# A three-block decoder on one core: every third Mamba state's product with B moved to GpSimd, from a copy of B in SBUF, with a new order table

## The chip, the cores and the metric

The kernel runs on one core of one Trainium2 chip. The metric is device time in microseconds (us), from the start of the program to its end. A profiled execution gives a trace with every instruction; its span is from the first to the last instruction.

## The reference

Four batches of 512 tokens of width 128 go through six blocks, each followed by a layer norm: a Mamba block, a cross attention of 16 heads, a mixture of experts, a window attention, a second cross attention, and a block of two layers of local attention with a gated feed-forward. The change lies in the Mamba block, whose scan is this:

```python
def step(h, inp):
    d_t, b_t, c_t, u_t = inp
    dA = jnp.exp(d_t[..., None] * A)
    dBu = d_t[..., None] * b_t[:, None, :] * u_t[..., None]
    h = dA * h + dBu
    y_t = jnp.einsum('bdn,bn->bd', h, c_t)
    return (h, y_t)
```

There are 256 channels and 16 states (index n). For each state the decay is exp(delta * A), the input is (delta * u) * B with B of that state, and the output adds h * C with C of that state.

## The kernel before

**Lanes and rounds.** The work of four batches is done in two lanes with buffers of their own (row buffers 0 and 1). Each lane computes two batches, one after the other (two rounds), and each batch goes through the six blocks. The two lanes run side by side: on each engine one instruction stream holds both lanes' instructions. Stage functions such as `mamba_tensor`, `mamba_scalar`, `mamba_vector` and `mamba_pool` are Python generators; each `yield` ends a step. `interleave` merges the lanes' steps by the table `TURNS`, which has a list of numbers for each engine: so many steps of lane 0, then so many of lane 1, and so on. The engines run their streams strictly in order, and semaphores tie them together. So `TURNS` is an order written out as numbers, for the whole kernel, and any new step in a lane shifts what the numbers mean behind it.

**The state loop.** Channels are two blocks (c = 0, 1) of 128 partitions; time (512 tokens) lies along the free axis. For each state n and each lane:

- TensorE spreads B of the state over all partitions (line 617, a selecting matmul of bf16 parts into PSUM), and later C of the state in the same way. Both go through one PSUM bank per lane (`t.v.use(1)`), so C can be written only when B has been read, and the next B only when C has been read.
- VectorE multiplies delta*u by B out of PSUM, both blocks in one instruction of 128x1024 (line 757), into `dBu[n % 2]`.
- ScalarE makes the decay exp(delta*A) of block 0 into one PSUM bank per lane (line 693, `dA`); VectorE runs the scan of block 0 (line 765, 128x512), which frees `dA`; then the same for block 1. So a lane's second exponential waits for its first scan, and the first of the next state for its second scan.
- ScalarE copies C out of PSUM into `Cs[n % 2]` (line 699).
- GpSimd multiplies the states of both blocks by C (line 796, 128x1024) into `hC[n % 2]`.
- TensorE adds `hC` to the sums in PSUM by two fp32 matmuls with the identity (line 623), which the trace shows as four records.

Buffers `hs`, `dBu`, `Cs` and `hC` are double: the scan of state n waits for GpSimd's product of state n-2, GpSimd's product of state n for the sum of n-2.

In the unrolled table of before, once the loop is under way, VectorE has two products (one of each lane) and then four scans, and so on. TensorE has, in the same stretch: C of one lane, C of the other, two sums, B of one, B of the other.

Behind the loop, lines 772 and 776 finish a lane's output, line 634 projects it, line 561 adds the residual; ahead of it, lines 741 to 746 make delta and delta*u. Later stages that the prediction speaks of: the cross attention behind Mamba (line 812 is its first matmul), the experts (lines 919, 963, 1008), the window attention (line 1115).

Of the kernel before, what the change touches and what calls it, by code (L numbers as in the profile page):

```python
# [32 lines left out]
P = 128  # L33
# [12 lines left out]
DEPTH = 2  # L46
EPS = 1e-5
# [35 lines left out]

TURNS = {
# [17 lines left out]
    "act": [  # L102
# [13 lines left out]
    "dve": [  # L116
# [21 lines left out]
    "pool": [  # L138
# [103 lines left out]
def decoder_kernel(nc, x_in, packed, cb_in, experts_in, folded_dram, out):  # L242
    with ExitStack() as ctx:
# [27 lines left out]
        def again(of, at=0):  # L271

            used[of] = at
# [1563 lines left out]
```

## Time and profile before

| | us |
|---|---|
| median of three runs | 1657.88 |
| lowest and highest of these | 1654.49 and 1671.53 |
| the profiled execution, its own time | 1675.55 |
| its span | 1673.8 |
| TensorE busy in it | 1360.8 (81%) |
| VectorE busy | 1076.3 (64%) |
| ScalarE busy | 807.2 (48%) |
| GpSimd busy | 328.3 (20%) |
| mean granted TensorE clock | 0.909 |

The shares are means over stages with different limits. The granted clock is given as a share of 2.4 GHz: 1.00 is 2.4 GHz all the time, 0.50 is 1.2 GHz. Lines of a trace name an instruction by its line in the kernel; "scratch" is the large SBUF buffer that holds most tiles of the stages.

### The profile page before, as it was taken

Reading aid. Unit: us, or ns where it says so; the run is one execution under the profiler, and the core shown is the slowest. Engines: PE = TensorE matmul, PEld = TensorE weight load, DVE = VectorE, ACT = ScalarE, POOL = GpSimd, SP = SyncE. Lnnn points to the kernel's source line nnn. Section 1 sums busy time; section 2 is a strip of 40 time slices with the busy share of each in tenths; the row PEclk is TensorE's granted clock in tenths of the full one; section 3 lists DMA queues with packets and bytes.
Section 4 is the critical chain, followed back from the end, with each engine's and each line's share of the span. In section 5 each row is a group of like instructions: output and inputs, shape, how many; then the busy total and the mean of one; then the engine's idle time right before and its main releaser. Section 6 shows DMA issues by size and latency. Waiting matters only on the chain. (4 is left out here: it accounts for less than half of the span.)

```text
span 1673.8 us, 23084 instructions
## 1 busy us (share of the span) xinstructions
PE 1360.8 (81%) x8604; PEld 858.4 (51%) x8604; DVE 1076.3 (64%) x2223; ACT 807.2 (48%) x2040; POOL 328.3 (20%) x212
## 2 busy tenths in 40 slices
PE   6656778998899789788865766899979986878886
PEld 5212235776566446455631223467756654654672
DVE  5599964115687788357439898721378877843863
ACT  0555414432666256546526452343347635664663
POOL 0046620002000052033010565100110004202310
PEclk9769968999999989989877899899999998999798
DMA  7300000000000010001000000000000000100000
GB/s 290 151 0 1 0 1 26 0 1 1 1 2 2 7 39 20 1 13 27 1 25 1 0 1 1 13 14 1 1 1 2 2 1 14 24 3 13 14 14 13
DMA packets 12927, 30.89 MB, mean 18 GB/s; under 512 B 1425, under 2 KB 5905, under 8 KB 12562
## 3 DMA queue, kind: packets, MB, share of 16 engines
q1 hardware_dynamic: 8978, 23.14, 3.7%
q10 hardware_dynamic: 3840, 6.29, 1.6%
q8 instruction: 69, 1.13, 0.3%
q14 instruction: 40, 0.33, 0.1%
HBM read 17.89 MB, written 5.24 MB: 14 GB/s over the span
## 5 line engine op out<-in xcount | busy, mean ns | idle before, releaser
L796 POOL TENSOR_TENSOR scratch<-scratch 128x1024 f32<-128x1024 f32 x64 | 149.4, 2352 | 174.8 <-DVE scratch L765 170.6
L963 ACT ACTIVATE scratch<-psum,w_experts 128x512 f32<-128x512 f32 x144 | 98.0, 688 | 146.1 <-PE psum L919 142.6
L535 POOL TENSOR_SCALAR rstd<-mv 128x4 f32<-128x4 f32 x28 | 7.7, 274 | 814.9 <-DVE mv L522 814.9
L693 ACT ACTIVATE psum<-scratch,a_neg 128x512 f32<-128x512 f32 x128 | 88.6, 692 | 129.7 <-DVE scratch L765 124.0
L765 DVE TENSOR_TENSOR_SCAN scratch<-psum,scratch 128x512 f32<-128x512 f32 x128 | 147.4, 1206 | 2.4 <-ACT psum L693 2.3
L1008 DVE SCALAR_TENSOR_TENSOR y<-psum,comb,y 128x128 f32<-128x128 f32 x128 | 36.0, 345 | 169.8 <-PE psum L943 169.8
L943 PEld LDWEIGHTS psum<-expert_weights,scratch 128*128 128x128 f32 x1152 | 134.1, 192 | 17.6 <-issue 17.1
L623 PE MATMUL psum<-scratch,w_const 128*128 128x512 f32 x256 | 134.6, 668 | 8.7 <-POOL scratch L796 8.6
L943 PE MATMUL psum<-expert_weights,scratch 128*128 128x128 f32 x1152 | 135.3, 275 | 0.9 <-DVE y L1008 0.9
L919 PE MATMUL psum<-xT,expert_weights 128*128 128x512 f32 x288 | 134.8, 602 | 1.1 <-ACT scratch L963 1.1
L1447 ACT ACTIVATE scratch<-psum,mx 128x128 f32<-128x128 f32 x256 | 90.3, 375 | 89.1 <-DVE mx L1538 89.0
L617 PE MATMUL psum<-scratch,cb 96*128 96x512 bf16 x128 | 49.0, 417 | 90.4 <-DVE scratch L757 74.5
L1115 ACT ACTIVATE scratch<-psum,mx 128x256 f32<-128x256 f32 (+1 forms) x256 | 111.3, 458 | 20.4 <-DVE mx L1151 18.6
L1282 PE MATMUL psum<-w_local,hT 128*128 128x512 f32 x192 | 93.4, 631 | 7.3 <-ACT hT L1264 7.1
L536 POOL TENSOR_TENSOR small<-small,w_const 128x16 f32<-128x16 f32 x32 | 96.1, 3004 | 2.7
L623 PEld LDWEIGHTS psum<-scratch,w_const 128*128 128x128 f32 x256 | 53.8, 215 | 64.7 <-issue 45.6
L617 PEld LDWEIGHTS psum<-scratch,cb 96*128 96x128 bf16 x128 | 12.7, 100 | 141.0 <-DVE scratch L757 101.1
L757 DVE TENSOR_TENSOR scratch<-scratch,psum 128x1024 f32<-128x1024 f32 x64 | 75.6, 1213 | 11.6 <-PE psum L617 11.6
L1325 PE MATMUL psum<-scratch 64*64 64x128 f32 x512 | 81.7, 308 | 0.0
L1323 PE MATMUL psum<-scratch 64*64 64x128 f32 x512 | 81.7, 308 | 0.0
L535 POOL TENSOR_SCALAR small<-small 128x16 f32<-128x16 f32 x32 | 24.0, 750 | 293.9 <-DVE small L1492 293.9
L1151 DVE TENSOR_REDUCE mx<-psum 128x4 f32<-128x1024 f32 (+1 forms) x56 | 68.4, 1222 | 15.8 <-PE psum L1062 15.7
(228 smaller groups left out, 3070.3 us busy)
## 6 DMA issues: line engine op xcount, KB each, us to landing
scratch<-scratch ACTq DMA_DIRECT2D x48, 128.0 KB, 2.3
expert_weights<-in_expert_weights SPq DMA_DIRECT2D x9, 512.0 KB, 9.8
folded_products<-scratch SPq DMA_DIRECT2D x8, 512.0 KB, 2.7
folded<-folded_products SPq DMA_DIRECT2D x8, 512.0 KB, 3.4
w_local<-in_local SPq DMA_DIRECT2D x1, 3122.0 KB
scratch<-in_cross SPq DMA_DIRECT2D x1, 2624.5 KB, 8.9
x<-in_x SPq DMA_DIRECT2D x4, 256.0 KB, 3.5
out<-xT SPq DMA_DIRECT2D x4, 256.0 KB, 2.4
```

Of the source, the lines that this page charges most:

```text
L536: t.eng.tensor_tensor(dst, dst, W("const", "neg_half").to_broadcast([P, dst.shape[1]]), ALU.pow)\
L623: ins = pe.matmul(sum_banks[c], ident, t.m.hC[:, 2 * ((n - 1) % 2) + c, :], start=(n == 1), stop=(n == NS))
L693: act.activation(t.ps["dA"], t.m.delta[:, c, :], ACT.Exp, scale=a_neg[:, c, n:n + 1])\
L765: dve.tensor_tensor_scan(t.m.hs[:, n % 2, c, :], t.ps["dA"], t.m.dBu[n % 2][:, c, :], 0.0, ALU.mult, ALU.add)\
L796: t.eng.tensor_tensor(t.m.hC[:, 2 * (n % 2):2 * (n % 2) + 2, :], t.m.hs[:, n % 2], C, ALU.mult)\
L919: pe.matmul(t.a.open(), we[:, k, f * P:(f + 1) * P], t.m.xT[:, :], start=True, stop=True)\
L943: ins = pe.matmul(tok(bank, i), tok(t.m.hid[:, (k - 1) % 2, f, :], i), we[:, k - 1, FF + f * P:FF + (f + 1) * P], start=(k > 1 and i == 0 ...
L963: act.activation(t.m.hid[:, k % 2, f, :], t.a.take(), ACT.Gelu_apprx_tanh, bias=W("experts", "b1")[:, c:c + 1]).then_inc(t.s["a_freed"], 1)
L1115: ins = act.activation(t.m.wide_pr[:, n % 2, u, z], bank[:, z], ACT.Exp, bias=t.m.mx2[:, c:c + 1], accum_out=t.m.sums2[:, c:c + 1])
L1282: pe.matmul(ring.open(), tok(t.m.hT, i), w_qkv[:, c * 512:(c + 1) * 512], start=True, stop=True).then_inc(t.s[sig], 1)
L1323: pe.matmul(own[0:64, :], qs[:, 0:64], ks[:, q - before:q - before + P], start=False, stop=False, skip_group_check=True)
L1447: ins = act.activation(tok(t.m.pr[:, u, :], a), tok(bank, a), ACT.Exp, bias=t.m.mx2[:, c:c + 1], accum_out=t.m.sums2[:, c:c + 1])
```

## The change

For the states 2, 5, 8, 11 and 14 the product with B is taken from VectorE and given to GpSimd. GpSimd reads B from SBUF, so ScalarE first copies B out of PSUM into a new tile `Bs` (one per lane). In GpSimd's stream the product of state n+1 stands ahead of the product h*C of state n. In ScalarE's stream the copy of B stands ahead of the state's first exponential, and for every state the copy of C now stands between the two exponentials (before: behind both). A new semaphore `B_used` tells VectorE's scan and ScalarE's next copy of B that GpSimd's product is done. `TURNS` is new for all four engines and the whole kernel, both rounds.

```diff
+POOL_B = range(2, NS, 3)
...
+            m.Bs = carve(i, 1, T)
...
# mamba_scalar
             for n in range(NS):
+                if n in POOL_B:
+                    yield
+                    if n > POOL_B[0] or t.row:
+                        t.w(t.s["B_used"])
+                    act.activation(t.m.Bs[:, 0, :], t.v.take(), ACT.Copy).then_inc(t.s["v_freed"], 1)
+                else:
+                    t.skip(v=1)
                 for c in range(NB):
...
-                t.skip(v=1)
-                yield
-                if n >= 2:
-                    t.w(t.s["state_ready"])
-                act.activation(t.m.Cs[:, n % 2, :], t.v.take(), ACT.Copy).then_inc(t.s["v_freed"], 1)
+                    if c == 0:
+                        yield
+                        if n >= 2:
+                            t.w(t.s["state_ready"])
+                        act.activation(t.m.Cs[:, n % 2, :], t.v.take(), ACT.Copy).then_inc(t.s["v_freed"], 1)
# mamba_vector
-                if n >= 2:
-                    dve.wait_ge(t.s["decay_used"], NB * (NS * t.row + n - 1))
-                bank = t.v.take().rearrange("p (o z) -> p o z", o=1).to_broadcast([P, NB, T])
-                dve.tensor_tensor(t.m.dBu[n % 2], t.m.du[:, :, :], bank, ALU.mult).then_inc(t.s["v_freed"], 1)
+                if n in POOL_B:
+                    t.skip(v=1)
+                else:
+                    if n >= 2:
+                        dve.wait_ge(t.s["decay_used"], NB * (NS * t.row + n - 1))
+                    bank = t.v.take().rearrange("p (o z) -> p o z", o=1).to_broadcast([P, NB, T])
+                    dve.tensor_tensor(t.m.dBu[n % 2], t.m.du[:, :, :], bank, ALU.mult).then_inc(t.s["v_freed"], 1)
                 for c in range(NB):
-                    yield
+                    if c or n not in POOL_B:
+                        yield
                     if c == 0:
-                        dve.wait_ge(t.s["v_freed"], t.v.at)
+                        if n in POOL_B:
+                            t.w(t.s["B_used"])
+                        else:
+                            dve.wait_ge(t.s["v_freed"], t.v.at)
# mamba_pool
+            def product_B(n):
+                yield
+                if n == POOL_B[0]:
+                    t.w(t.s["delta_ready"])
+                t.eng.wait_ge(t.s["v_freed"], t.v.at + 1)
+                t.eng.wait_ge(t.s["decay_used"], NB * (NS * t.row + n - 1))
+                t.eng.tensor_tensor(t.m.dBu[n % 2], t.m.du, t.m.Bs.to_broadcast([P, NB, T]), ALU.mult)\
+                    .then_inc(t.s["B_used"], 1)
             for n in range(NS):
                 t.skip(v=2)
+                if n + 1 in POOL_B:
+                    yield from product_B(n + 1)
```

Unrolled, the new table gives these streams in the middle of the loop (first round, three states of both lanes). The digit ahead is the lane, the number the state; P is line 757, s a scan with its block a or b, e an exponential, C and BS the copies, hC and PB GpSimd's products with C and B, b TensorE's spreading of B (a) or C (b), sum line 623:

```
VectorE  1s8b 1P9 0s10b 1s9a 1s9b 1P10 0s11a 1s10a 0s11b 0P12 1s10b 0s12a 0s12b 0P13 1s11a 0s13a 1s11b
GpSimd   0hC9 1hC8 0PB11 0hC10 1hC9 0hC11 1PB11 1hC10 0hC12 1hC11
ScalarE  0BS11 1C9 0e11a 0C11 1e9b 1e10a 1C10 0e11b 1e10b 0e12a 1BS11 0C12 1e11a 1C11 0e12b 0e13a
TensorE  1b10a 1b10b 0sum10 0b12a 1sum9 1b11a 0b12b 1b11b 0sum11 0b13a 0b13b 1sum10 1b12a 0sum12
```

## Rows read from the trace of the kernel before

**Rows 1.** Busy time of each engine, stretches of the two state loops
```profile
core 0: us, PE busy (x) PEld busy (x) DVE busy (x) ACT busy (x) POOL busy (x), PEclk, DMA share, GB/s
120.00:160.00 40.00, 27.91 (x69) 10.63 (x68) 38.36 (x35) 21.11 (x36) 26.08 (x12) 0.97 0.00 1
...
960.00:1000.00 40.00, 27.50 (x71) 10.86 (x71) 40.00 (x37) 21.68 (x36) 27.32 (x12) 1.00 0.00 1
```

**Rows 2.** Timeline of VectorE, one period (start, length, line, count)
```profile
151.44 2.35 DVE L757 TENSOR_TENSOR scratch<-scratch,psum 128x1024 f32<-128x1024 f32 x2
153.70 4.56 DVE L765 TENSOR_TENSOR_SCAN scratch<-psum,scratch 128x512 f32<-128x512 f32 x4
158.21 1.22 DVE L757 TENSOR_TENSOR scratch<-scratch,psum 128x1024 f32<-128x1024 f32 x1
```

**Rows 3.** Timeline of TensorE, the same period
```profile
153.84 0.39 PE L617 MATMUL psum<-scratch,cb 96*128 96x512 bf16 x1 [0.74 <-DVE scratch L757]
154.07 3.60 PE L623 MATMUL psum<-scratch,w_const 128*128 128x512 f32 x8
157.50 0.60 PE L617 MATMUL psum<-scratch,cb 96*128 96x512 bf16 x2
```

**Rows 4.** Timeline of VectorE, fourth to fifteenth state of both rounds
```profile
115.94 2.33 DVE L757 TENSOR_TENSOR scratch<-scratch,psum 128x1024 f32<-128x1024 f32 x2
124.39 2.35 DVE L757 TENSOR_TENSOR scratch<-scratch,psum 128x1024 f32<-128x1024 f32 x2 [1.64 <-PE psum L617]
...
193.50 2.33 DVE L757 TENSOR_TENSOR scratch<-scratch,psum 128x1024 f32<-128x1024 f32 x2
...
933.26 2.33 DVE L757 TENSOR_TENSOR scratch<-scratch,psum 128x1024 f32<-128x1024 f32 x2
...
943.03 2.35 DVE L757 TENSOR_TENSOR scratch<-scratch,psum 128x1024 f32<-128x1024 f32 x2 [2.96 <-PE psum L617]
...
1012.33 2.35 DVE L757 TENSOR_TENSOR scratch<-scratch,psum 128x1024 f32<-128x1024 f32 x2
```

**Rows 5.** Busy time and clock, two stretches of 4 us
```profile
120.00:124.00 4.00, 4.00 (x8) 1.41 (x7) 2.75 (x3) 3.05 (x6) 2.29 (x1) 0.68 0.00 0
936.00:940.00 4.00, 4.00 (x6) 1.69 (x5) 4.00 (x4) 2.92 (x5) 1.94 (x2) 0.50 0.00 0
```

**Rows 6.** Timelines of GpSimd and ScalarE in the loop
```profile
136.96 4.67 POOL L796 TENSOR_TENSOR scratch<-scratch 128x1024 f32<-128x1024 f32 x2 [2.11 <-DVE scratch L765]
134.68 0.69 ACT L693 ACTIVATE psum<-scratch,a_neg 128x512 f32<-128x512 f32 x1 [2.74 <-DVE scratch L765]
135.31 0.58 ACT L699 ACTIVATE scratch<-psum 128x512 f32<-128x512 f32 x1
135.80 0.69 ACT L693 ACTIVATE psum<-scratch,a_neg 128x512 f32<-128x512 f32 x1
```

**Rows 7.** Timeline of VectorE where line 746 meets GpSimd's first product
```profile
89.81 1.22 DVE L744 TENSOR_TENSOR scratch<-scratch 128x1024 f32<-128x1024 f32 x1
95.45 2.48 DVE L746 TENSOR_TENSOR scratch<-scratch 128x1024 f32<-128x1024 f32 x1
```

**Rows 8.** Stage ends by line, first round (to 906), then second (ns; first and last start)
```profile
L765 DVE TENSOR_TENSOR_SCAN scratch<-psum,scratch x64: 1194/1202/1224, 91.0 to 212.0; 128x512 f32<-128x512 f32 x64
L1008 DVE SCALAR_TENSOR_TENSOR y<-psum,comb,y x64: 339/344/352, 297.2 to 408.5; 128x128 f32<-128x128 f32 x64
L1115 ACT ACTIVATE scratch<-psum,mx x128: 358/473/547, 427.7 to 543.0; 128x256 f32<-128x256 f32 x96, 128x128 f32<-128x128 f32 x32
...
L765 DVE TENSOR_TENSOR_SCAN scratch<-psum,scratch x64: 1193/1201/1224, 908.8 to 1030.4; 128x512 f32<-128x512 f32 x64
L1008 DVE SCALAR_TENSOR_TENSOR y<-psum,comb,y x64: 335/344/352, 1103.1 to 1220.2; 128x128 f32<-128x128 f32 x64
L1115 ACT ACTIVATE scratch<-psum,mx x128: 359/474/548, 1235.7 to 1346.6; 128x256 f32<-128x256 f32 x96, 128x128 f32<-128x128 f32 x32
```

More of the change, by code:

```diff
@@ L387, in decoder_kernel @@
                      "stats_ready rstd_ready norm_ready score_loaded e_ready prob_ready pT_used x_loaded "
-                     "squares_ready rms_ready u_ready soft_ready delta_ready parts_ready decay_ready decay_used state_ready states_used "
+                     "squares_ready rms_ready u_ready soft_ready delta_ready parts_ready decay_ready decay_used state_ready states_used B_used "
                      "sum_filled sums_read gated_ready gap_ready ratio_ready comb_ready pads_ready "
```

106 rows, old and new, of the table TURNS are left out of this document.

## Prediction

> **What bounds the kernel now.** The change lies in the state loop, which runs twice, once a round; so I read the busy time of each engine in stretches of the loop first, where the page's shares over the whole span would mislead. VectorE works 38.36 of 40 us in the first round's loop and 40.00 of 40 in the second's; TensorE is at 28, GpSimd at 26 and 27, ScalarE at 21 [rows 1]. That says VectorE. The timeline of one period says how closely another bound follows. A period is one state of both lanes: two products with B, then four scans, from 151.44 to 158.21, so 6.77 us, with no idle time between them [rows 2]. The steps between starts are 1.13 for a product and 1.128 for a scan: (158.21 - 153.70) / 4. Beside it runs a chain through TensorE: the second product ends at 151.44 + 2.35 = 153.79, TensorE starts C at 153.84, the eight records of the two sums from 154.07, the next two B at 157.50, which take 0.60 [rows 3]; that ends at 158.10, and the next product starts at 158.21. So product, C, two sums, B and product again also make 6.77. The loop has two bounds of one length, and taking away VectorE's work alone frees only one of them.
>
> The second one shows where the granted clock falls. From the fourth state's pair of products to the fifteenth's are 193.50 - 115.94 = 77.56 us in the first round and 1012.33 - 933.26 = 79.07 in the second, for 11 states each [rows 4]: 7.05 and 7.19 a state, and not 6.77. Two of the stalls stand in the rows, 1.64 and 2.96 us, both on line 617; the granted clock in the stretches ahead of them is 0.68 and 0.50 [rows 5], so wholly or partly at 1.2 GHz. Over 22 states this costs 156.63 - 22 x 6.77 = 7.7 us.
>
> **The change, by the engine's own work.** I count three states of both lanes, since the pattern repeats after three; one round has five such patterns and a state more.
>
> VectorE now has 6 products and 12 scans, 6 x 1.13 + 12 x 1.128 = 20.3 us. Two products go: 18.05. Over both rounds 5 states x 2 lanes x 2 = 20 products go, 22.6 us of VectorE. That is the most which VectorE's own work can give.
>
> GpSimd has 6 products with C; two back to back take 4.67 [rows 6], 2.335 each. The new product has the same shape, 128x1024 fp32 from two SBUF operands, so I take the same duration. Eight make 18.7 us: GpSimd, that idled a third of the time, becomes the fullest engine, above VectorE's 18.05. Nothing shorter than 18.7 is possible.
>
> ScalarE has 12 exponentials at a step of 0.63 and 6 copies at 0.49 (135.31 - 134.68 and 135.80 - 135.31) [rows 6], 10.5 us; two more copies of B make 11.5. It doesn't fill up, but its stream is in order, which matters next.
>
> **The change, by what waits for what.** I laid the four new streams side by side and followed who must wait. GpSimd's product of lane 1's state 8 waits for that state's second scan. Behind it, in one stream, are lane 0's product with B of state 11, lane 0's product with C of state 10 and lane 1's product with C of state 9: four in a row. The last of them is awaited by TensorE's sum of state 9 of lane 1, and TensorE's spreading of B for state 11 of lane 1 stands behind that sum. On it waits ScalarE's copy of B, and behind the copy in ScalarE's stream stand the copy of C of lane 0's state 12, lane 1's exponential of 11, a copy of C, and the second exponential of lane 0's state 12. On that waits VectorE's scan; behind that scan stand lane 0's product 13, lane 1's scan of 11, lane 0's of 13, and the second scan of lane 1's state 11, for which GpSimd waits in turn. So the circle closes after three states. Its length:
>
> - GpSimd: 4 x 2.335 = 9.34 [rows 6]
> - TensorE: four records of a sum at (157.50 - 154.07) / 8 = 0.43, 1.72, and B, 0.39: 2.11 [rows 3]
> - ScalarE: 0.49 + 0.49 + 0.63 + 0.49 + 0.69 = 2.79 [rows 6]
> - VectorE: a scan, a product and two scans by their steps, 4.51, and the last scan in full, about 1.18: 5.69 [rows 2]
> - four hand-overs between engines: 0.05 (153.79 to 153.84) and 0.11 (158.10 to 158.21) are the two seen [rows 2, 3]; at 0.08 each, 0.3
>
> Sum 20.2 us for three states, 6.75 a state, beside 6.77 now. GpSimd then idles 1.5 us in three states and VectorE 2.2, though neither has a lack of work. So at the full clock I expect the loop not to gain from the 22.6 us that VectorE sheds: the wait for the product with B is replaced by one for GpSimd, handed on through sum, B and copy.
>
> What does gain is the loop's dependence on TensorE's clock. Now the circle holds a C, two sums and two B a period, all twice as long at 1.2 GHz, some 4.2 us in 6.77, 12.7 in three states; after the change 2.1 in 20.2. If the clock dips as it does now, the 7.7 us shrink by 2.1 / 12.7, to about 1.3. For the 22 states: 22 x 6.75 + 1.3 = 149.8 instead of 156.6, -6.8 us.
>
> The other ten states (the first four of each round, and the last) run with parts of the prologue and at a low clock. The new streams start with a product with B of state 2 ahead of GpSimd's product with C of state 1: late for lane 0's sum, early for its scan. I take nothing, with bounds of 3 us either way a round (half a period).
>
> The copy of C between the exponentials costs its 0.49 us ahead of each second exponential, but that one waits for its first scan (2.74 us of idle time before an exponential [rows 6]), so it lies in idle time: nothing, and up to 0.5 a state if that cover is gone; it gives C to GpSimd about one exponential earlier, for which nothing waits.
>
> One place costs. Line 746 took 2.48 us at 95.45, its like, line 744, 1.22 at 89.81 [rows 7]; GpSimd's first product ran in the same time. After the change GpSimd has a second product right behind it. Between nothing and 2.3 us a round, I take 0.5, so +1.0.
>
> By the Trainium skill ("SBUF — State Buffer", Who interferes with whom) a VectorE instruction with two SBUF inputs blocks against a GpSimd instruction that reads SBUF, and one with at most one SBUF input doesn't. By that rule line 746 may be held once more, and the scans and products of the loop, whose other input is in PSUM, never are. The trace agrees as far as GpSimd is now busy: the scans stay within 1.193 to 1.224 us in all 128 [rows 8]. If a fuller GpSimd held them up all the same, the loop would be slower than I say.
>
> **The order elsewhere.** The table is new for the whole kernel, and nothing else changes there. What an order can do is seen in the trace itself, since the two rounds do the same work by different lists. From the last scan to the experts' last instruction are 408.5 - 212.0 = 196.5 us in the first round and 1220.2 - 1030.4 = 189.8 in the second; the window attention from there 134.5 and 126.4 [rows 8]. I compared the lists by counting, for each step of lane 1, the steps of lane 0 ahead of it. In the window attention the new lists of both rounds lie within 1 to 2 steps of the old second round's on ScalarE and VectorE, and 3 to 6 from the old first round's. So the first round may gain up to 8.1 us there. Part of it is chance of the clock; I take half, -4. In cross attention and experts the new lists on TensorE lie nearer to the old first round's (some 5 steps) than to the second's (some 14), so the second round may lose up to 6.7; but the experts fill TensorE whatever the order. I take nothing, with bounds of -7 and +7.
>
> **Sum.** -6.8 + 1.0 - 4 = -9.8 us. Against the profiled execution's own 1675.55 (span 1673.8 and 1.75 around it) this gives 1665.7. That execution lies 17.7 us above the median of the runs, 1657.88; the same difference on the median gives 1648.1, my forecast. About 1% (16.6 us) is what a measurement of this kernel can tell from no change, since three runs before spread over 17 us.
>
> **The rivals.**
>
> *GpSimd is the bound, not the circle.* If hand-overs are shorter than I sum, or the streams slip against each other so that copy and sum are met earlier, three states take 18.7, 6.23 a state. Then 22 x (7.12 - 6.23) = 19.6 us go, and at half of that a state for the other ten, 4.5: with the window's -4 and the +1, 1631. For it: GpSimd's stream needs only 1.5 us less waiting in three states. Against it: each step of the circle is a fixed place in an in-order stream.
>
> *The new order elsewhere is worse.* The lists differ most in cross attention and experts. If both rounds lose there what now separates the rounds, 2 x 6.7 = 13.4, and the window gains nothing, then 1657.9 - 6.8 + 1 + 13.4 = 1665.5. It decides from about 6 us of loss. For it: the second round's list, the better one, is given up. Against it: TensorE is nearly full there.
>
> *Waits grow on the way.* If each hand-over costs 0.3 us instead of 0.08 (GpSimd's are seen on no tight path here), the circle is 21.1, 7.04 a state, and the loop gains 1.7 us over 22 states: 1653.
>
> **How the numbers follow.** Forecast 0.43, GpSimd the bound 0.27, the order worse 0.18, longer waits 0.12. The range 1626 to 1671 reaches past the first rival on one side (start of the loop 3 us a round better) and past the second by a part of its bounds on the other. Faster by over 1% means under 1641.3: nearly all of the first rival and a little of the forecast, 0.32. Slower by over 1% means over 1674.5: the tail of the second, 0.11. Within 1%: 0.57.
>
> **What would show it.** In the changed kernel's trace: GpSimd's busy time up by 20 x 2.35 = 47 us, to about 375; VectorE's down by about 24. From pair to pair three states apart 20.2 us if the circle holds, 18.7 if GpSimd is the bound: then its timeline has products without idle time. The waits should show the sum (line 623) waiting for GpSimd, line 757 no longer for line 617, and VectorE idle about 2 us in three states. The stage ends of rows 8 tell the order's part: the first round's window attention should be near 130. Wrong it would be if the loop's 11 states take under 72 us or over 78, or if the stages outside move by over 10 us in sum.

## The result, and the profile after

The changed kernel takes 1674.01 us, median of 16 runs (1659.67 to 1680.51); the kernel before 1662.32 in 16 runs of its own. The ratio is 1.0054, with a 95% interval of 1.0034 to 1.0075: slower by half a per cent, some 9 us, where I had forecast 9.8 us faster. The median lies above my range of 1626 to 1671. Part of that is the starting point: the forecast stood on three runs with a median of 1657.88, and 16 runs of the same kernel now give 4.4 us more. The direction was wrong all the same.

The page of the changed kernel gives for each engine its busy time, its share of the span and its number of instructions (PEld is TensorE loading weights):

```profile
PE 1375.6 (82%) x8604; PEld 867.0 (52%) x8604; DVE 1053.1 (63%) x2203; ACT 821.4 (49%) x2060; POOL 378.5 (23%) x232
```

The move did what it says. VectorE has 20 instructions and 23.2 us less, GpSimd 20 more and 50.2 us more, ScalarE 20 copies more. TensorE is the odd one: the same 8604 matmul records, and 14.8 us more in them (13.7 in the second profiles of both, told of below).

The page's groups of the loop (busy, mean ns | idle time ahead and what ended it); line 829 is GpSimd's product with C, 786 the scan, 630 the sum, 707 the exponential, 624 the spreading of B and C:

```profile
L829 POOL TENSOR_TENSOR scratch<-scratch 128x1024 f32<-128x1024 f32 x64 | 151.2, 2379 | 95.6 <-DVE scratch L786 95.5
L786 DVE TENSOR_TENSOR_SCAN scratch<-psum,scratch 128x512 f32<-128x512 f32 x128 | 150.0, 1209 | 26.1 <-ACT psum L707 25.4
L630 PE MATMUL psum<-scratch,w_const 128*128 128x512 f32 x256 | 142.0, 683 | 14.3 <-POOL scratch L829 13.0
L707 ACT ACTIVATE psum<-scratch,a_neg 128x512 f32<-128x512 f32 x128 | 88.5, 693 | 51.6 <-DVE scratch L786 48.9
```

The page of the kernel before has this for the scan:

```profile
L765 DVE TENSOR_TENSOR_SCAN scratch<-psum,scratch 128x512 f32<-128x512 f32 x128 | 147.4, 1206 | 2.4 <-ACT psum L693 2.3
```

VectorE idled 2.4 us ahead of scans and now idles 26.1 us, waiting for exponentials. That is 23.7 us more, about what it has given away (22.6 us of products).

The stage ends by line, as in [rows 8], first round and then second:

```profile
L786 DVE TENSOR_TENSOR_SCAN scratch<-psum,scratch x64: 1191/1214/1225, 88.6 to 205.1; 128x512 f32<-128x512 f32 x64
L1041 DVE SCALAR_TENSOR_TENSOR y<-psum,comb,y x64: 335/343/352, 290.6 to 404.5; 128x128 f32<-128x128 f32 x64
L1148 ACT ACTIVATE scratch<-psum,mx x128: 357/472/543, 419.8 to 533.0; 128x256 f32<-128x256 f32 x96, 128x128 f32<-128x128 f32 x32
...
L786 DVE TENSOR_TENSOR_SCAN scratch<-psum,scratch x64: 1191/1216/1225, 900.0 to 1020.8; 128x512 f32<-128x512 f32 x64
L1041 DVE SCALAR_TENSOR_TENSOR y<-psum,comb,y x64: 336/343/351, 1114.9 to 1220.4; 128x128 f32<-128x128 f32 x64
L1148 ACT ACTIVATE scratch<-psum,mx x128: 357/472/545, 1235.8 to 1350.1; 128x256 f32<-128x256 f32 x96, 128x128 f32<-128x128 f32 x32
```

From the last scan to the experts' end are 404.5 - 205.1 = 199.4 us and 199.6, against 196.5 and 189.8 before. The window attention takes 128.5 and 129.7, against 134.5 and 126.4.

One profile of a kernel is one execution, so I took a second of each. In this table every stretch is worked out from the stage ends as above: "loop" is from the first product with B of lane 0 to the start of the last scan, "to experts' end" from there to the start of the experts' last instruction.

| us | loop, round 1, 2 | to experts' end | window | span |
|---|---|---|---|---|
| before, two profiles | 124.6, 123.9; 122.5, 123.6 | 196.5, 189.8; 193.8, 189.7 | 134.5, 126.4; 134.5, 125.8 | 1673.8; 1664.8 |
| changed, two profiles | 120.0, 123.0; 119.8, 123.2 | 199.4, 199.6; 199.4, 199.5 | 128.5, 129.7; 128.5, 129.7 | 1672.8; 1666.2 |

The changed kernel's stretches come again to 0.2 us; of the kernel before, the first round's loop and the stretch behind it differ by 2.1 and 2.7 us. The local layers further on differ more (in the first round 276.3 and 271.2 us before, 281.2 and 274.3 changed). In the mean of two profiles the spans of the two kernels are equal (1669.3 and 1669.5), so single profiles can't carry a difference of 9 us; the runs do.

### The profile page after: what moved, and what is told of

Same layout as the page of the kernel before. It is cut to its first block and busy times, and to the rows that moved or that the text cites. A ratio compares the mean times of both kernels' runs of the same rounds, so it can differ in the third digit from the quotient of the medians.

```text
span 1672.8 us, 23122 instructions
## 1 busy us (share of the span) xinstructions
PE 1375.6 (82%) x8604; PEld 867.0 (52%) x8604; DVE 1053.1 (63%) x2203; ACT 821.4 (49%) x2060; POOL 378.5 (23%) x232
## 5 line engine op out<-in xcount | busy, mean ns | idle before, releaser
L786 DVE TENSOR_TENSOR_SCAN scratch<-psum,scratch 128x512 f32<-128x512 f32 x128 | 150.0, 1209 | 26.1 <-ACT psum L707 25.4
L630 PE MATMUL psum<-scratch,w_const 128*128 128x512 f32 x256 | 142.0, 683 | 14.3 <-POOL scratch L829 13.0
L976 PEld LDWEIGHTS psum<-expert_weights,scratch 128*128 128x128 f32 x1152 | 137.7, 196 | 15.3 <-issue 14.8
L976 PE MATMUL psum<-expert_weights,scratch 128*128 128x128 f32 x1152 | 138.6, 280 | 0.0
L1315 PE MATMUL psum<-w_local,hT 128*128 128x512 f32 x192 | 99.5, 666 | 6.8 <-ACT hT L1297 6.4
L952 PEld LDWEIGHTS psum<-xT,expert_weights 128*128 128x128 f32 x288 | 51.2, 190 | 50.0 <-issue 45.8
L624 PEld LDWEIGHTS psum<-scratch,cb 96*128 96x128 bf16 x128 | 13.1, 102 | 123.0 <-DVE scratch L774 71.7
## 6 DMA issues: line engine op xcount, KB each, us to landing
x<-in_x SPq DMA_DIRECT2D x4, 256.0 KB, 3.5
out<-xT SPq DMA_DIRECT2D x4, 256.0 KB, 2.4
```

What stands on the lines that cost most here:

```text
L630: ins = pe.matmul(sum_banks[c], ident, t.m.hC[:, 2 * ((n - 1) % 2) + c, :], start=(n == 1), stop=(n == NS))
L786: dve.tensor_tensor_scan(t.m.hs[:, n % 2, c, :], t.ps["dA"], t.m.dBu[n % 2][:, c, :], 0.0, ALU.mult, ALU.add)\
L952: pe.matmul(t.a.open(), we[:, k, f * P:(f + 1) * P], t.m.xT[:, :], start=True, stop=True)\
L976: ins = pe.matmul(tok(bank, i), tok(t.m.hid[:, (k - 1) % 2, f, :], i), we[:, k - 1, FF + f * P:FF + (f + 1) * P], start=(k > 1 and i == 0 ...
L1315: pe.matmul(ring.open(), tok(t.m.hT, i), w_qkv[:, c * 512:(c + 1) * 512], start=True, stop=True).then_inc(t.s[sig], 1)
```

## The experiments

Each run is compared with the kernel before on the same chip, by 4 to 11 executions of the edited kernel; the runs came in four batches on four chips, and ratios of different batches are compared only by way of the kernel before.

**Splitting order and loop.** Three kernels take the old order in one part and the new one in the other. Nothing but the numbers of `TURNS` differs.

```diff
 e1: TURNS: new inside both state loops, old everywhere else (changed code)
 e2: TURNS: old inside both state loops, new everywhere else (code before)
 e3: TURNS: new, but old in cross attention and experts      (changed code)
```

> The changed kernel with its new order only inside the two state loops; ahead of, between and behind them the four engines keep the old order. Theory A (the loop gains a little, the new order elsewhere costs more): from the first product with B to the last scan 120 to 123 us a round (124.6 and 123.9 before), the stretch from the last scan to the experts' last instruction back at about 196 and 190 us (199.4 and 199.6 in the changed kernel), and the whole faster than the kernel before, ratio 0.994 to 0.999. Theory B (the loop itself is what costs, or the two profiles differ by the clock alone): ratio near 1.005, as the changed kernel.

> The other half: the kernel before with its old code and old order in the state loops, and the new order everywhere else. Theory A: slower than the kernel before by more than the changed kernel is, ratio 1.006 to 1.012, with the last scan to the experts' end at 199 us in both rounds. Theory B: ratio 1.000 within 0.002.

> The changed kernel with the old order in cross attention and experts alone (both rounds); loops, window attention and all behind it keep the new order. Theory A in its narrow form (the cost sits in cross attention and experts, 2.9 and 9.8 us in the two profiles): ratio 0.996 to 1.000, the stretch at about 196 and 190 us. If the cost of the new order is spread over the later stages: ratio 1.003 or above.

> The kernel before once more, for a second profile of it. If stage lengths are set by the order, each stretch between stage ends comes again within 2 us of the first profile (loop 124.6 and 123.9, cross attention and experts 196.5 and 189.8, window 134.5 and 126.4). If they are set by when the clock falls, they scatter by as much as the two kernels differ (3 to 10 us).

Measured: the new loop in the old surroundings 1.0054 (1.0027 to 1.0080), the old loop in new surroundings 1.0042 (1.0017 to 1.0067). Each half alone costs about half a per cent, and both together, the changed kernel, no more than one of them. So the parts don't add. Theory A, as I had put it, falls by the first run (0.994 to 0.999 expected) and misses the second (1.006 to 1.012); Theory B falls by the second, since it wanted 1.000 there. Both the loop with its hand-over and the order elsewhere cost something by themselves. With the old order in cross attention and experts alone the ratio is 1.0191 (1.0165 to 1.0217), where 0.996 to 1.000 was expected. The stretch in question takes 201.5 and 196.3 us there, and the window attention goes to 138.6 and 140.6: two good lists don't make one when they are joined.

The loops take 120.7 and 116.2 us in the first of these kernels and 121.9 and 116.5 in the second, the stretches to the experts' end 198.7 and 197.0, and 196.3 and 196.5 (199 was expected). But that stretch starts with lane 1's last scan, and cross attention with lane 0, whose residual starts 1.5 us ahead of that scan in the kernel before (first round), 6 behind it in the changed one and 9 and 10 in the first of these. So the stretch gets longer when only lane 1 ends earlier, and loop and stretch are better taken together. These windows of the second round run from the first product to the experts' end; they have each engine's busy time (with its number of instructions), the granted clock, the DMA share and GB/s. The kernel before, the changed one, the new loop in the old surroundings, the old loop in the new ones:

```profile
core 0: us, PE busy (x) PEld busy (x) DVE busy (x) ACT busy (x) POOL busy (x), PEclk, DMA share, GB/s
906.50:1220.20 313.70, 255.94 (x1136) 154.02 (x1137) 190.15 (x374) 125.64 (x197) 87.78 (x49) 0.93 0.01 4
897.80:1220.40 322.60, 266.09 (x1132) 157.98 (x1132) 178.23 (x357) 132.15 (x207) 112.09 (x59) 0.90 0.01 4
903.60:1216.80 313.20, 256.89 (x1136) 153.88 (x1137) 175.94 (x360) 130.57 (x205) 110.70 (x59) 0.92 0.01 4
896.00:1209.00 313.00, 252.89 (x1132) 152.34 (x1132) 185.48 (x365) 123.97 (x195) 88.29 (x49) 0.94 0.01 4
```

The second profiles of the first two have the same within 0.4 us (313.3 and 322.7). Neither half alone makes the second round longer up to here; only both together do, by 9 us, and TensorE is busy 10 us longer over the same work: the loss is its clock (0.90 against 0.93), not waiting. In the first round all four are alike (316.4 to 321.1 before, 319.4, 319.5, 318.1). Where each half alone loses its half per cent these single profiles don't show; up to here it isn't.

The loop itself takes as long in either form when the clock is the same: lane 0's 11 states from product 4 to 15 took 76.3 us in the new loop and 75.9 in the old one, both at 0.96 from 20 to 60 us behind the first product. In the changed kernel they took 80.3 at 0.79, in the kernel before 79.1 at 0.87.

**The parts, one at a time.**

```diff
 e5 (code and order before): only the copy of C between the exponentials
 e7 (order of the changed kernel): products with B back on VectorE, no Bs
 e4 (changed kernel, mamba_tensor):
-                    for which in (n, NS + n):
+                    for which in ((NS + n,) if n in POOL_B else (n, NS + n, n + 1) if n + 1 in POOL_B else (n, NS + n)):
```

> One part alone: the kernel before, with its old order, in which ScalarE copies C between a state's two exponentials; all products with B stay on VectorE. I expect nothing: ratio 1.000 within 0.002, a period of 6.75 us in the loop. If this part is what costs (the second exponential behind a wait for C), the loops are longer by 0.2 us or more a state and the ratio is 1.003 or above.

> The changed kernel's whole order, but the twenty products with B back on VectorE (each right behind the lane's last scan) and no copies of B. If moving the products gains in the loop, this one is slower than the changed kernel: its period is at least 6.77 us a state as before, so 3 to 8 us slower in sum, ratio to the kernel before 1.007 to 1.010. If the loop has gained nothing by the move and the new order alone makes the difference, the ratio is 1.004 to 1.006, as the changed kernel's.

> The changed kernel, but for the states whose product is on GpSimd TensorE spreads B ahead of the sum that stood before it, so that ScalarE's copy of B no longer waits for that sum and for GpSimd's product ahead of it. If the circle GpSimd, sum, B, copy, exponential, scan is what sets the pace (20.2 us in three states), it is opened, and the next one is close: three states in 19.7 us, the loop 1 to 2 us shorter a round, the whole 2 to 4 us faster than the changed kernel (ratio to the kernel before 1.002 to 1.004). If GpSimd's own work or something else set the pace, three states still take 20.2 us.

> The changed kernel once more, for a second profile. What the order sets should come again within 2 us: loop 120.0 and 123.0, the last scan to the experts' end 199.4 and 199.6, window attention 128.5 and 129.7. The local layers (281.2 and 271.0) I expect to scatter by 5 us, as in the kernel before.

> The run with B ahead of the sum once more, for its ratio (0.9967 with 0.9940 to 0.9994) and for a second profile: loops within 2 us of 119.3 and 115.3, last scan to the experts' end of 194.9 and 195.0. If the second round's 115.3 was luck of the clock, it comes as 120 or more now.

The copy of C costs nothing: 1.0002 (0.9972 to 1.0031). The new order without the move is slower than with it: 1.0093 (1.0062 to 1.0124), with loops of 128.9 and 128.3 us. By the two ratios, moving the products is worth about 0.4% in that order, and the order had taken more than that away; the intervals overlap (1.0034 to 1.0075 and 1.0062 to 1.0124), so the size isn't firm, but the loops, 5 to 9 us longer, point the same way.

B ahead of the sum opens the circle (the sum of GpSimd's, TensorE's, ScalarE's and VectorE's steps that closes after three states). VectorE's timeline of the changed kernel, lane 0's products 9, 12 and 15 of the second round:

```profile
965.78 1.20 DVE L774 TENSOR_TENSOR scratch<-scratch,psum 128x1024 f32<-128x1024 f32 x1
...
985.98 1.20 DVE L774 TENSOR_TENSOR scratch<-scratch,psum 128x1024 f32<-128x1024 f32 x1
...
1006.19 1.20 DVE L774 TENSOR_TENSOR scratch<-scratch,psum 128x1024 f32<-128x1024 f32 x1
```

and of the kernel with B ahead, products 10 and 13 of lane 0 in the first round:

```profile
156.64 1.20 DVE L774 TENSOR_TENSOR scratch<-scratch,psum 128x1024 f32<-128x1024 f32 x1
...
176.36 1.20 DVE L774 TENSOR_TENSOR scratch<-scratch,psum 128x1024 f32<-128x1024 f32 x1
```

20.20 and 20.21 us against 19.72, as expected (19.7). That is 0.5 us in three states, and it holds where the clock is 1.00: the second round has 19.73 twice, but other groups of three states in the same trace, at a mean clock of 0.90 to 0.92, take 21.1 and 22.0. Even so the whole gained more. The ratio is 0.9967 (0.9940 to 0.9994), and 1.0000 (0.9977 to 1.0024) the second time, against 1.0054 for the changed kernel; the two intervals overlap, so I take it as no slower than the kernel before. Both its profiles (spans 1650.0 and 1650.7, both among the fastest executions of their runs, whose medians are 1653.96 and 1661.84) show loops of 119.3 and 115.3 and 119.4 and 115.3 us, and a stretch to the experts' end of 194.9 and 195.0 us, twice. An edit worth 2 us by the circle shortened the second loop by 8 and the stretches behind by 4.5 each, and it came again to a tenth. The greater part of the 8 isn't the circle's: lane 0's 11 states went from 80.3 to 75.0 us, and without the edit, in the old surroundings, they took 76.3.

**The clock.** Windows with the same columns (the granted clock is the third number from the end), second round, from 20 to 60 us behind the first product; first the kernel before, then the changed one, then B ahead:

```profile
926.50:966.50 40.00, 28.53 (x61) 10.94 (x61) 35.55 (x33) 18.76 (x31) 23.58 (x11) 0.87 0.00 0
```

```profile
917.80:957.80 40.00, 31.67 (x64) 11.97 (x62) 31.06 (x28) 20.07 (x33) 30.45 (x14) 0.79 0.00 0
```

```profile
905.20:945.20 40.00, 30.21 (x74) 11.33 (x73) 35.83 (x32) 24.53 (x40) 36.37 (x16) 0.96 0.00 0
```

In the changed kernel TensorE is busy longest, with fewer records in the same time (64, against 74 with B ahead): it is partly at 1.2 GHz. And the stretch from the last scan to the experts' end, the changed kernel's second round and that with B ahead, again second round:

```profile
1020.80:1220.40 199.60, 178.72 (x946) 126.08 (x946) 75.19 (x267) 66.34 (x100) 16.83 (x18) 0.92 0.02 6
```

```profile
1000.50:1195.50 195.00, 175.50 (x948) 122.92 (x946) 75.01 (x267) 66.46 (x100) 16.85 (x18) 0.94 0.02 6
```

The order in it is the same in both kernels, and so are VectorE's, ScalarE's and GpSimd's busy times within 0.2 us. TensorE is busy 3.2 us longer, of 4.6 in all. In windows of 4 us, first round, the granted clock of the changed kernel is still 0.50 here:

```profile
232.00:236.00 4.00, 3.98 (x10) 1.91 (x9) 3.13 (x6) 1.89 (x3) 0.00 (x0) 0.50 0.00 0
236.00:240.00 4.00, 4.00 (x9) 2.01 (x8) 1.38 (x3) 0.00 (x0) 0.00 (x0) 0.50 0.00 0
```

and that of the kernel with B ahead at the same place (its cross attention starts 1 us earlier) is 0.94 and 1.00. It had fallen earlier, for as long (0.50 from 216 to 232 us, in the changed kernel from 224 to 240), when TensorE had less to do: 10.5 us busy in those 16, against 14.4:

```profile
232.00:236.00 4.00, 3.98 (x15) 1.90 (x14) 3.18 (x6) 1.45 (x3) 0.00 (x0) 0.94 0.00 0
236.00:240.00 4.00, 3.88 (x21) 2.42 (x21) 3.90 (x9) 1.71 (x3) 0.00 (x0) 1.00 0.01 2
```

So I changed TensorE's activity alone: by doubled matmuls in the loop, and by a filler, four matmuls whose result nothing uses, in the gap in which TensorE waits for VectorE's norm ahead of lane 0's first cross attention.

```diff
 e8 (changed kernel, mamba_tensor): each spreading matmul twice while n < 8
 e13 (changed kernel), e14 (the run e9 below), cross_tensor:
+            if inner and t.m is rows[0]:
+                bank = t.a.open()
+                for k in range(4):
+                    pe.matmul(bank, ident, W("local", "w_qkv")[:, 0:T], start=True, stop=True)
+                t.a.at -= 1
             t.w(t.s["norm_ready"], 2 if inner else 1)
```

> The changed kernel, but TensorE does each spreading of B and of C twice for the first eight states of both rounds (the same matmul into the same bank), 0.22 us more work each at the full clock. If the second round's loop (123.0 and 123.2 us in two profiles, granted clock 0.77 to 0.84 in its first half) is long because TensorE falls to 1.2 GHz in its gaps, more activity keeps the clock up: granted clock 0.95 or more in that half, loop 116 to 119 us in the second round, and a ratio below 1.004. If the clock is not what makes it long, the doubled work only lengthens the circle: loops 2 to 4 us longer in both rounds, ratio 1.007 or more.

The first half of the second loop, which was at 0.79:

```profile
921.80:961.80 40.00, 33.72 (x92) 12.66 (x90) 33.51 (x30) 23.04 (x39) 33.69 (x16) 0.96 0.00 1
```

Clock 0.96, and that loop went from 123.0 to 119.9 us in spite of 0.22 us more work in each spreading; the first loop, whose clock had been better, became longer (122.7). The loop is a little longer than the 116 to 119 us expected. The ratio is 1.0019 (0.9994 to 1.0044), below 1.004 as the clock theory had it. From the first product to the experts' end the second round takes 318.0 us instead of 322.7, the first 320.9 instead of 319.4. The interval overlaps the changed kernel's, so that the clock's effect is shown in the second round, and less surely in the whole.

**Easing the circle further.** With B ahead, I interleaved the lanes' steps in the two loops anew, from the same rows and the same kind of sum as in the prediction; and as a counterpart took the same order with the products back on VectorE.

```diff
 e9:  e4, TURNS new inside both state loops
 e12: the order of e9, products with B on VectorE, no Bs
```

> B ahead of the sum as in the run before, and in the two state loops the lanes' steps interleaved anew on all four engines, so that no product of GpSimd, sum or copy stands in front of one that is needed earlier; the work of each engine is the same, outside the loops the changed kernel's order stands. With the circle gone GpSimd is the bound, 18.7 us in three states: loops of 111 to 115 us instead of 119.3 and 115.3, ratio to the kernel before 0.988 to 0.993. If handing over between engines costs more than I count, loops of 117 us or more and no gain on the run before.

> The same eased order in the loops, but the twenty products with B back on VectorE, no copies of B. VectorE's own work is then 6.77 us a state: loops of 119 to 124 us, 7 to 10 us longer a round than with the products on GpSimd in the same order, ratio 1.000 to 1.006. If the eased order were what helps and not the moved products, this one would be as fast.

Loops of 113.7 and 116.4 us, and a ratio of 0.9962 (0.9938 to 0.9986); with the products on VectorE 129.6 and 120.4 us and 1.0116 (1.0083 to 1.0148). In this order the moved products are worth 16 and 4 us a round, 1.5% in all. That isn't a gain on the kernel before, since the order was made for the moved products: without them it is itself 1.2% slower than the kernel before, and slower than I expected. Against the kernel before, the eased kernel gains 0.4%, no more than B ahead alone did, where 0.7 to 1.2% was expected. GpSimd's bound of 18.7 us in three states was reached in one group of lane 0 (18.4, clock 1.00), while others at a clock of 0.75 to 0.85 took 22.4 and 23.3. And the stretch to the experts' end went back to 200.2 and 199.6 us, with TensorE 181.1 us busy in the first. The filler goes for that.

> The changed kernel, and ahead of lane 0's first cross attention TensorE does four idle matmuls of 128x512 fp32 into the bank that the transposes then overwrite, about 3.4 us of filler in a gap of 4.2 us in which it waits for VectorE's norm. If the fall of the clock in that gap is what costs (0.50 from 222 to 241 us), the clock stays at 0.9 or more there, the stretch from the last scan to the experts' end goes from 199.4 and 199.6 us to 193 to 196, and the ratio to 0.999 to 1.002. If the order costs and the clock doesn't, the stretch stays at 199 or gets longer by the filler, ratio 1.005 or more.

> The eased loop order with the same filler. If the clock's fall there costs 4 to 5 us a round as in the changed kernel, the stretches go from 200.2 and 199.6 us to about 195 and the ratio from 0.9962 to 0.990 to 0.993. If the filler only stands in the way, 0.997 or more.

In the changed kernel it failed: 1.0074 (1.0044 to 1.0104), stretches of 198.5 and 197.4 us. The clock was better where the filler stood (0.85 from 222 to 228 us, 0.50 there without it) and fell elsewhere. A window of the first round, where the experts begin:

```profile
264.00:268.00 4.00, 4.00 (x12) 2.87 (x12) 1.96 (x17) 1.17 (x2) 1.24 (x2) 0.50 0.00 0
```

In the eased kernel it did what was expected: ratio 0.9897 (0.9861 to 0.9933, five executions), loops of 116.8 and 113.1, stretches of 193.1 and 193.2 us. First without, then with the filler:

```profile
198.20:398.40 200.20, 181.09 (x947) 126.79 (x946) 75.19 (x267) 66.55 (x100) 16.84 (x18) 0.91 0.02 6
```

```profile
202.00:395.10 193.10, 175.92 (x955) 122.58 (x954) 75.06 (x268) 66.44 (x100) 16.83 (x18) 0.96 0.02 6
```

More matmuls, 5.2 us less of busy TensorE, 7.1 us less in all. This kernel, at 1642.47 us against 1662.17 on the same chip, beats both that the study began with. That the same filler works in one order and not in the other shows how little one gap can be treated by itself. The filler was never put into the kernel before, so how much of the 1% it would have given there is open.

## Why the prediction was wrong

- **Engines' own work: right.** VectorE 23 us less, GpSimd 50 more (forecast 24 and 47), the new product 2.35 us.
- **The circle: right at the full clock.** 20.2 us in three states forecast, 20.20 and 20.21 measured where the clock is 1.00, and opening it at the place named gave the 19.7 expected there. VectorE's and GpSimd's spare time went into the waits named. The first rival, GpSimd as the bound, did not come true.
- **"If the clock dips as it does now, the 7.7 us shrink ... to about 1.3": the step of the loop that failed.** The dips were to cost 1.3 us over 22 states, since only 2.1 us of TensorE's work lie in the circle. Lane 0's products 4, 6 and 15 (1006.19, the second round's product 15, stands above):

```profile
113.81 1.20 DVE L774 TENSOR_TENSOR scratch<-scratch,psum 128x1024 f32<-128x1024 f32 x1
...
190.51 1.20 DVE L774 TENSOR_TENSOR scratch<-scratch,psum 128x1024 f32<-128x1024 f32 x1
...
925.91 1.20 DVE L774 TENSOR_TENSOR scratch<-scratch,psum 128x1024 f32<-128x1024 f32 x1
...
943.36 1.22 DVE L774 TENSOR_TENSOR scratch<-scratch,psum 128x1024 f32<-128x1024 f32 x1 [1.69 <-PE psum L624]
```

That is 76.7 and 80.3 us for 11 states, 157.0 in all; forecast 149.8, before 156.6. The second one is outside the 72 to 78 that I had set. At the circle's pace 22 states are 148.1 us, so 8.9 us were lost over the pace and not 1.3. In the second round product 4 to 6 took 17.5 us at a mean clock of 0.74, 6 to 9 22.4 at 0.90, and from 9 on 20.2 at 1.00. I had priced only the matmuls in the circle, but TensorE is busy 14.7 of the 20.2 us at the full clock, and at 1.2 GHz its own stream would take some 29 (an estimate, twice 14.7): then TensorE is the bound again. No run tests that estimate by itself. The dip was also deeper, 0.79 instead of 0.87 in the window above; why isn't shown. In the old surroundings, at 0.96, the same loop took 76.3. The two loops by their ends (lane 1's) gained 3.7 and 0.7 us in the mean of two profiles.
- **Lane 0 was overlooked.** I summed a loop, and not who ends when. Lane 0's residual (line 561, now 568) starts 210.5 - 87.4 = 123.1 us behind the first product before, and 211.2 - 85.1 = 126.1 after; in the second round 126.4 and 129.1. The leading lane is 3 us later, lane 1 (138.7 to 134.2) earlier, and cross attention starts with lane 0.
- **"In cross attention and experts ... I take nothing": the term that was furthest off.** It measured +4.3 and +9.8 us in the mean of the profiles, with bounds of 7 either way set for it. Part of it is only where the stretch starts: from lane 0's residual on, it is 193.5 us instead of 187.3 in the second round and 193.3 instead of 198.0 and 195.3 in the first. But from the first product to the experts' end, where forecast were -6.8 for both rounds, it is +0.5 and +9.2 in the mean of two profiles. The 9.2 are TensorE's clock: its busy time goes from 256.0 to 266.1 us there. Of the 6.2 us from lane 0's residual on, 175.0 - 170.9 = 4.1 are its busy time; the other 2.1 are idle time, which the old loop in the new surroundings has as well for the most part (18.5 us idle here, 19.2 there, 16.4 before), so that they go with the order. With the same lists B ahead takes 3 us a round away from lane 0's residual on (190.4 and 190.6), and the filler in the eased kernel 7.1 and 4.8. "The experts fill TensorE whatever the order" was nearly true, and left out that the clock may not be full.
- **The window attention: -4 forecast.** Measured -6.0 and +3.6, -2.4. The first round moved as read off the lists; that the second would lose, although its lists moved by 1 to 2 steps only, I had not seen.
- **Line 746** (760 in the changed kernel) took 2.48 us again in both rounds, as before; GpSimd's second product came only later. The +1.0 was nothing. The other side of it, which I hadn't counted, shows at 206.40: a product of GpSimd beside line 797 of the changed kernel, a product of VectorE with two SBUF inputs, took 3.24 us instead of 2.35.

The second rival was the one closest to the time, with its price of 13.4 us in cross attention and experts (14.1 measured), and I had given it 0.18. That its price fits so well is partly luck: it had 6.7 us in each round, by the order alone, and measured are 4.3 and 9.8, with the clock and the shifted start in them; the order alone makes nothing up to the experts' end. What stays open: where the 9 us of the runs lie. Up to the experts' end the profiles show 9.7 us and the window attention takes off 2.4, but over the whole they show nothing, since the first round's local layers scatter by 5 to 7 us between two profiles of the same kernel and the second round's were some 6 us shorter in the changed one.

## What to carry to other kernels

When work is moved off a full engine in a kernel of in-order streams, add up the longest circle through all engines after the move, and look for a place where a fetch for later stands behind a sum for earlier: one pair of steps exchanged there turned a loss of 0.5% to none or a small gain. An order fitted to the move and a filler brought 1.0% on the kernel before, the order without the filler 0.4%. Sum it for each lane's end, since the next stage starts with the first lane and not with the last. And where TensorE idles in gaps, compare its busy time for the same instructions before believing that a stage is untouched: it tells the clock's part from the order's, which shows as idle time.

## What was not expected of the hardware

TensorE's clock is neither pure chance nor fixed by the program. Two profiles of the changed kernel, and two of that with B ahead, show the same dips at the same places (0.79 and 0.79 in the window from 20 to 60 us behind the first product, the changed kernel; 0.96 and 0.96 with B ahead), and stretches that agree to 0.2 us. The two kernels differ by one pair of steps in the order, and from 232 to 240 us one is at 1.2 GHz and the other nearly all the time at 2.4. But the kernel before has 0.51 in one profile and 0.71 in the other from 135 to 155 us behind its first product. And the filler stands behind the first loop, so that up to there the programs are the same in order and work; even so that loop took 124.0 us with it against 120.0 and 119.9 (clock 0.81 against 0.92 in the same window), and in the eased kernel 116.8 against 113.7. So a difference of 3 or 4 us in a single loop of a single profile can be the clock's chance; the runs' intervals decide.

Extra matmuls can pay: four of 128x512 in one gap of each round went with 7.1 and 6.4 us less in the stretch behind it in one order, and with 0.9 and 2.2 in another.
